# A graph network kernel: a pipelined stage whose first and last passes run only their live operations, and a reordered last stage

## The chip, the cores and the metric

The kernel runs on one core of a Trainium2 chip. The metric is the device time of one launch in microseconds (us). Three launches of the kernel before took 1610.73, 1611.04 and 1617.06 us, so the median is 1611.04 us.

## The reference

The input is a graph of N = 50000 nodes with 128 features each (`x`), and E = 12500 edges (`src`, `dst`, sorted by `dst`) with 128 features each. Two blocks follow each other, each closed by a layer norm over the 128 features:

```
agg  = segment_sum(h[src], dst);  mean = agg / max(deg, 1)
sage(h)  = h @ W_self + mean @ W_neigh + b            # twice, with a relu between them
x1   = layernorm(x + sage(relu(sage(x))))
q,k,v = heads of x1 @ Wq, x1 @ Wk, x1 @ Wv;  e = edge_attr @ We          # H = 4 heads of 128
alpha = (q[dst] . (k[src] + e)) / sqrt(128);  attn = softmax of alpha over the edges of one dst
out  = segment_sum((v[src] + e) * attn, dst) + x1 @ Wskip + bskip
lin  = (layernorm(out) * ln_g + ln_b) @ Wlin + blin
y    = layernorm(x1 + elu(lin + x1))
```

Most nodes have no incoming edge. For them the mean and the attention sum are zero, and the result is a function of the node's own row alone.

## The kernel before, in words

The program has five stages, each a block in which SyncE (SP, issues transfers), GpSimd (POOL), TensorE (PE), ScalarE (ACT) and VectorE (DVE) run their own lists of instructions, with a barrier of all engines between two stages (`phase`, line 1906):

- **setup** (lines 314 to 638): loads and folds the weights, builds index tables from `dst` and `src`.
- **node stage** (`b_sync`, `b_pool`, `b_pe`, `b_act`, `b_dve`, lines 656 to 924): computes every node as if it had no edges, in blocks of 512 rows (NBLK = 98 blocks), and writes `x1` to a table and the final row to the output.
- **A** (line 992 on) and **C** (line 1115 on): the first block of the network for the nodes with edges, 98 tiles of 128 edges in 25 groups.
- **D** (`d_sync` to `d_dve`, lines 1331 to 1903): attention and the output of the nodes with edges, one tile of 128 edges a pass, with scatters over the output's rows; then one last tile for a node whose edges are split between tiles.

The node stage is a software pipeline. A pass `it` works on block `it - lag` in each step; the lags stand in `B_LAG` (line 652) and go from 0 (transpose of the loaded rows) to 6 (the output row `b_o`). NBLK = 98 and the largest lag 6 give TILES = 104 passes. PE, ACT and DVE run them in a hardware loop of 26 turns with four passes in each (lines 707, 753, 800), and in every pass they do every step, also where `it - lag` is no block: such a step works on memory that setup has cleared (lines 363, 515, 635), and its output, where it is stored at all, goes to the tensor `unused` (lines 661 to 680). Every step has a semaphore that starts at CREDIT = 16, so that waits for earlier passes are met at once.

A full pass has, per engine, in this order:

- PE: 4 transposes (L714), 8 products for `y` (L721, L722), 4 transposes of `x1` (L728), one product of 512 columns (L733), 4 products of 256 columns (L739), each wide product in several machine instructions.
- ACT: copy L759, exponential L763, half of the output rows L748, copy L772, relu L776, the other half of L748, Ln L784, Exp L788, and four scaled copies L794 that make `x1`.
- DVE: four sums of squares L807, four statistics L815 for the output (lag 5), clamp L819, four statistics L823 of the y product (lag 1), aggregates L827 and L831, `b_t` L835, `b_w` L839, four `b_z` L844, `b_nm3` L852.
- SP: the load of block `it + 2` (L668), the store of the output block (L672), the store of the `x1` block (L676).
- POOL: `b_x1c` (L880), then indirect transfers: a gather of node rows (L888, passes 0 to 98), and two of the scatters into `redirect` (L894) and, after those, of the look-ups from it (L861); in each sixth pass of the first 96 one of the two is replaced by a gather for stage A (L338). In passes 0, 4, 8, ... 48 it also issues one thirteenth of `dst_row`, the row of all `dst` indices repeated on 128 partitions and cast to 16 bits (L905), and before pass 0 it clears or fills seven tiles (L867 to L872).

In stage D a tile passes through lags too: `a` is the new tile (98 of them), `b` = `a` - 10 the tile whose values are weighted, `c` one behind `b`, `d` two behind. From pass 98 on (`a >= NT`) there is no new tile: this is the drain. In one pass ACT does `turned(c)` (L1591 copy, L1593 square), `exponential(d)` (L1599), `weighted(b)` (L1577, four), L1635, then L1639 and L1641 (the inverse deviation of the output row), L1650 (the output row of `d`), and L1661, L1663 (the inverse deviation for `c`, on which `d_z` L1791 of the next pass waits). DVE's last two steps in a drain pass are `d_nm2` L1830 and `d_var` L1780, and the latter waits for a product of PE (L1457) that stands behind the products L1436 and L1423.

## Time and profile before

| what | us |
|---|---|
| median of three launches | 1611.04 |
| the profiled launch, device time | 1612.87 |
| its span, first to last instruction | 1610.7 |
| setup, to the first load of the node stage | 0 to 34.7 |
| node stage, to the first instruction of stage A | 34.7 to 646.7 |
| stage A | 646.7 to 799.4 |
| stage D's drain and its last tile | 1522 to 1610.7 |

A line of the timeline gives the start in us, the duration in us, the engine, the line, the operation, what it writes and reads, how many instructions are merged in the line, and in brackets how long the engine had been idle before and what ended that. "SPq" and "PEq" are an engine's queue of issued work. An engine that is idle is no loss unless it is the one that the others wait for, so the rows are read for who waits.

### The profile page before, as it was taken

What the parts mean: (1) busy time and instruction counts of PE and PEld (TensorE: products, weight loads), DVE (VectorE), ACT (ScalarE), POOL (GpSimd) and SP (SyncE); (2) the same over time, 40 slices, a digit from 0 to 9 for tenths busy, and PEclk for the clock granted to TensorE, in tenths of its full rate; (3) what the DMA queues carried; (4) which work ended last, traced back from release to release, by engine and by line L of the source; (5) the groups of instructions that cost most, each with busy time, mean ns of one, the idle gap of its engine ahead of it and who ended that gap; (6) DMA issues with size and microseconds to landing.
All of it is one profiled execution on the core that took longest, in us unless ns stands there. A gap on an engine that the chain in (4) does not pass through costs nothing. (4 is left out here: it accounts for less than half of the span.)

```text
span 1610.7 us, 35668 instructions
## 1 busy us (share of the span) xinstructions
PE 1483.8 (92%) x8869; PEld 1135.5 (70%) x8869; DVE 1326.6 (82%) x6248; ACT 1169.2 (73%) x3273; POOL 1036.0 (64%) x1038
## 2 busy tenths in 40 slices
PE   4999999999999998999699977999999999999973
PEld 3777777777777776788566643777777777777763
DVE  5999999999999998566468865788888888888873
ACT  2999999999999998344257751677777777777763
POOL 3788888878888885677367727466566556655421
PEclk9999999999999999999989998999999999999997
DMA  2566666554444443233269963233333333333210
GB/s 80 147 161 159 159 162 162 155 159 150 150 150 150 152 150 119 73 92 92 58 197 288 291 214 97 81 91 91 90 89 87 88 91 90 90 90 88 67 41 6
DMA packets 148429, 199.22 MB, mean 124 GB/s; under 512 B 28399, under 2 KB 71582, under 8 KB 148310
## 3 DMA queue, kind: packets, MB, share of 16 engines
q1 hardware_dynamic: 119690, 160.01, 32.5%
q0 software_dynamic: 27200, 36.26, 10.0%
q10 hardware_dynamic: 1420, 1.60, 0.3%
q8 instruction: 46, 0.75, 0.2%
q14 instruction: 73, 0.60, 0.2%
HBM read 106.66 MB, written 100.07 MB: 128 GB/s over the span
## 5 line engine op out<-in xcount | busy, mean ns | idle before, releaser
L1371 POOL DMA_INDIRECT big<-x_tab,look x196 | 199.8, 1019 | 92.3 <-issue 58.6
L739 PEld LDWEIGHTS pb<-MG_s,big 128*128 128x128 f32 x832 | 149.5, 189 | 126.7 <-ACT big L772 110.5
L1388 POOL DMA_INDIRECT out_dram<-big,idx x98 | 100.5, 1026 | 210.6 <-PE pb L1466 73.4
L739 PE MATMUL pb<-MG_s,big 128*128 128x256 f32 x832 | 207.3, 392 | 24.7 <-ACT big L772 24.6
L748 ACT ACTIVATE big<-big 128x128 f32<-128x128 f32 x416 | 180.2, 482 | 0.0
L721 PE MATMUL pb<-C_s,big 128*128 128x128 f32 x832 | 161.8, 276 | 0.0
L722 PE MATMUL pb<-Ws1c_s,big 128*128 128x128 f32 x832 | 161.8, 276 | 0.0
L880 POOL TENSOR_TENSOR big<-big,cl 128x512 f32<-128x512 f32 x104 | 133.3, 1282 | 36.1 <-DVE big L844 34.0
L1689 DVE CUSTOM_DVE_ANT_0 big<-pb,big,zero 128x128 f32<-128x128 f32 x392 | 119.6, 345 | 38.7 <-PE pb L1511 38.3
L1442 PEld LDWEIGHTS pb<-big 128*128 128x128 f32 x792 | 103.9, 192 | 51.8 <-issue 37.7
L1121 POOL DMA_INDIRECT big<-h1e_tab,hidx x98 | 98.1, 1001 | 60.0 <-issue 35.5
L861 POOL DMA_INDIRECT look<-redirect,idx x98 | 115.8, 1182 | 29.1 <-issue 28.0
L894 POOL DMA_INDIRECT redirect<-idx x98 | 114.7, 1170 | 30.3 <-issue 30.3
L338 POOL DMA_INDIRECT a_xs<-in_x_dram,idx x98 | 100.9, 1029 | 48.3 <-issue 35.9
L722 PEld LDWEIGHTS pb<-Ws1c_s,big 128*128 128x128 f32 x832 | 127.3, 193 | 0.0
L794 ACT ACTIVATE big<-pb,big 128x128 f32<-128x128 f32 x416 | 118.6, 368 | 11.8
L1429 PEld LDWEIGHTS pb<-big,Wskip_s 128*128 128x128 f32 x784 | 101.2, 191 | 36.8 <-issue 36.3
L721 PEld LDWEIGHTS pb<-C_s,big 128*128 128x128 f32 x832 | 127.1, 193 | 0.0
L807 DVE CUSTOM_DVE_ANT_0 big<-pb,big,zero 128x128 f32<-128x128 f32 x416 | 120.5, 346 | 1.9 <-ACTq L265 1.9
L1436 PE MATMUL pb<-big 128*128 128x128 f32 x784 | 112.0, 286 | 5.4 <-ACT big L1577 5.4
L844 DVE SCALAR_TENSOR_TENSOR big<-pb,big 128x128 f32<-128x128 f32 x416 | 116.5, 342 | 0.0
L1442 PE MATMUL pb<-big 128*128 128x129 f32 x792 | 106.4, 277 | 8.4 <-ACT big L1591 5.7
(362 smaller groups left out, 4165.8 us busy)
## 6 DMA issues: line engine op xcount, KB each, us to landing
big<-in_x_dram SPq DMA_DIRECT2D x104, 256.0 KB
x_tab<-big SPq DMA_DIRECT2D x98, 256.0 KB
out_dram<-big SPq DMA_DIRECT2D x98, 256.0 KB, 2.1
c_ve<-ve_tab SPq DMA_DIRECT2D x98, 256.0 KB, 2.6
ve_tab<-c_ve SPq DMA_DIRECT2D x66, 256.0 KB, 3.6
h1e_tab<-a_rows SPq DMA_DIRECT2D x25, 256.0 KB, 2.6
x_tab<-a_rows SPq DMA_DIRECT2D x25, 256.0 KB
big<-in_edge_attr_dram SPq DMA_DIRECT2D x97, 64.0 KB, 1.8
```

What stands on the lines that cost most here:

```text
L721: pe.matmul(o, b_xT[(u - 1) % 2][:, r * P:(r + 1) * P], C_s[:], start=True, stop=False)
L722: t = pe.matmul(o, b_h1T[:, r * P:(r + 1) * P], Ws1c_s[:], start=False, stop=True)
L739: t = pe.matmul(o, b_x1T[:, r * P:(r + 1) * P], MG_s[:], start=True, stop=True)
L748: return act.activation(b_o[u % 2][:, r * D:(r + 1) * D], b_w[u % 2][:, r * D:(r + 1) * D], ACT.Identity, scale=brs3[:, r:r + 1], bias=b_n ...
L794: t = act.activation(b_x1[(u - 1) % 4][:, r * D:(r + 1) * D], PY[(u - 1) % 2][:, r * D:(r + 1) * D], ACT.Copy, bias=1.0, scale=brs1[:, r:r ...
L807: t = v.tensor_tensor_reduce(b_junk[:, r * D:(r + 1) * D], PMG[(u - 3) % 2][r // 2][:, (r % 2) * 256 + 128:(r % 2) * 256 + 256], b_x1[(u - ...
L844: t = v.scalar_tensor_tensor(out=b_z[(u - 3) % 2][:, r * D:(r + 1) * D], in0=PMG[(u - 3) % 2][r // 2][:, (r % 2) * 256:(r % 2) * 256 + 128 ...
L861: g.indirect_dma_start(out=look[:, 0, e:e + 1], out_offset=None, in_=redirect, in_offset=bass.IndirectOffsetOnAxis(ap=idx[:, SRC, e:e + 1] ...
L880: g.tensor_tensor(b_x1c[u % 2].rearrange("p (r d) -> p r d", r=R), b_x1[(u - 2) % 4].rearrange("p (r d) -> p r d", r=R), cl[:].rearrange(" ...
L1371: g.indirect_dma_start(out=o, out_offset=None, in_=x1_tab, in_offset=bass.IndirectOffsetOnAxis(ap=look[:, a, j:j + 1], axis=0), bounds_che ...
L1442: t = pe.matmul(o, hs(ob, h), Wgc_s[:, h, :], start=(h == 0), stop=(h == H - 1))
L1689: return v.tensor_tensor_reduce(hs(junk, h), hs(logit_bank(a), h), d_x1d[a % XD], SCALE, zero[:, 0:1], ALU.mult, ALU.add, d_al[:, H * a + ...
```

## The change

- PE, ACT and DVE run the passes through `all_passes`: passes 0 to 7 and 92 to 103 are written out, with only the steps whose block exists (`present`); passes 8 to 91 stay in a loop of 21 turns of four. A wait for a step is capped at the last value that the step reaches (`due`), and each semaphore's start is raised by the step's lag, in place of the dead steps' increments.
- SP issues no store for a block that does not exist; the tensor `unused` is gone. SP now also waits at the stage's end until `dst_row` has landed.
- POOL runs 102 passes. In passes 2 to 99 it makes `b_x1c`; in every pass it issues three indirect transfers from one list: redirect and node row by turns (198), 16 gathers for stage A, 92 look-ups (91 before).
- The clearings of the node stage's memory are gone from setup (L363, L515, L635, with the waits of L632 and L633). The fills L867 to L872 and the transfers of `dst_row`, now 8 in place of 13 and a small rest, are in POOL's setup, the latter behind a wait for setup's last loads.
- Stage D, passes from 98 on: ACT's square L1593 comes behind the exponential L1599, and the output row L1650 behind L1661 and L1663; DVE's final sum (L1813 to L1821) comes right behind `d_z` and ahead of `d_same` L1798 and the sums L1769.

```diff
-            g.memset(big[:, b_second:b_small_end], 0.0)
+            g.memset(b_mv, 0.0)
+            g.memset(dst_row[:, E:TILES * P], NOWHERE)
+            for k in range(4):
+                g.memset(a_xs[k][:], 1.0)
+            for t in (a_mnT, a_colT, a_colH):
+                g.memset(t[:], 0.0)
+            g.wait_ge(s_ld, 16 * LOADS["later"])
+            part = E // PIECES
+            for k in range(PIECES):
+                at, n = k * part, part if k < PIECES - 1 else E - k * part
+                g.dma_start(dst_row[:, at:at + n], dst[at:at + n].rearrange("(a n) -> a n", a=1).to_broadcast([P, n])
+                            ).then_inc(s_row, 16)
+
+        PIECES = 8
...
-            v.memset(big[:, b_first:b_second], 0.0)
...
-            w("cl")
-            v.wait_ge(s_sa, am["skip"])
-            for b in pb[6:8]:
-                v.memset(b[:].rearrange("p (a d) -> p a d", a=2)[:, :, 0:D], 0.0)
...
+        def b_passes(name):
+            return NBLK + (B_LAG["b_nm3"] - B_LAG[name] if name in ("b_ln", "b_rs") else 0)
+        def present(name, it):
+            return not isinstance(it, int) or B_LAG[name] <= it < B_LAG[name] + b_passes(name)
+        def due(eng, name, value):
+            last = CREDIT + B_LAG[name] + b_passes(name)
+            eng.wait_ge(step(name), min(value, last) if isinstance(value, int) else value)
+        def credit(eng, names):
+            for n in names.split():
+                eng.sem_inc(step(n), CREDIT + B_LAG[n])
...
+        def all_passes(eng, turn):
+            for it in range(4 * EDGE):
+                turn(it, it % 4, it // 4)
+            with eng.Fori(EDGE, LOOPS) as i:
+                for u in range(4):
+                    turn(4 * i + u, u, i)
+            for it in range(4 * LOOPS, PASSES):
+                turn(it, it % 4, it // 4)
...
-                    pe.wait_ge(step("b_h1"), made(B_LAG, "b_h1", it, 1))
-                    pe.wait_ge(step("b_x1"), freed(B_LAG, "b_x1", it, 1, 2))
+                if present("b_py", it):
+                    due(pe, "b_h1", made(B_LAG, "b_h1", it, 1))
+                    due(pe, "b_x1", freed(B_LAG, "b_x1", it, 1, 2))
...
-            for it in range(TILES):
...
+            def move(m):
+                if m < 2 * (NT + 1):
+                    (node_row if m % 2 else redirect_rows)(m // 2)
+                elif m < LOOK_AT:
+                    gather_src(g, (m - 2 * (NT + 1)) // R, (m - 2 * (NT + 1)) % R)
+                else:
+                    if m == LOOK_AT:
+                        for k in range(4):
+                            g.wait_ge(dma_p[k], 16 * len(range(k, NT + 1, 4)))
+                    look_up(g, m - LOOK_AT)
+            for it in range(PASSES - 2):
+                if present("b_x1c", it):
+                    x1c(it, it % 4)
+                for m in range(3 * it, 3 * it + 3):
+                    move(m)
...
+                if live(c) and a < NT:
+                    squared(c)
                 if live(d):
                     exponential(d)
+                if live(c) and a >= NT:
+                    squared(c)
...
-                if live(d):
-                    after(act, "d_nm2", d)
...
+                if live(d) and a < NT:
+                    finished(d)
...
                     act.activation(d_rs[c % 2], d_lw, ACT.Exp, scale=-0.5).then_inc(step("d_rs"), 1)
+
+                if live(d) and a >= NT:
+                    finished(d)
...
+                if live(d) and a >= NT:
+                    final_sum(d)
 
                 if live(b):
                     v.tensor_scalar(d_same[b % 2], dst_row[:, b * P:(b + 1) * P], dst_f[:, b + 1:b + 2], None,
...
-                if live(d):
...
+                if live(d) and a < NT:
+                    final_sum(d)
```

## Rows read from the trace of the kernel before

**Rows 1.** The page, part 1: busy us, share of the span, instructions.

```profile
PE 1483.8 (92%) x8869; PEld 1135.5 (70%) x8869; DVE 1326.6 (82%) x6248; ACT 1169.2 (73%) x3273; POOL 1036.0 (64%) x1038
```

**Rows 2.** Windows: us, then PE, PEld, DVE, ACT, POOL busy (count), PEclk, DMA, GB/s.

```profile
34.70:47.20 12.50, 9.51 (x49) 8.63 (x50) 5.79 (x33) 5.63 (x15) 9.17 (x14) 0.73 0.46 110
...
605.60:611.40 5.80, 5.56 (x37) 4.48 (x36) 5.69 (x34) 5.49 (x15) 4.68 (x4) 1.00 0.43 144
```

**Rows 3.** The timeline, setup's end and the start of the node stage.

```profile
33.24 0.55 DVE L635 MEMSET pb<- 128x256 f32 x2
...
34.72 0.81 SPq L688 DMA_DIRECT2D big<-in_x_dram  x2
34.80 0.77 POOL L867 MEMSET dst_row<- 128x812 uint16 x1 [26.35 <-POOLq L1922]
```

**Rows 4.** The timeline, pass 0 of the node stage.

```profile
37.69 1.11 PE L714 MATMUL pb<-ident,big 128*128 128x128 f32 x4 [5.01 <-DMA big<-in_x_dram]
...
38.59 0.63 PE L721 MATMUL pb<-C_s,big 128*128 128x128 f32 x2
...
39.26 0.69 ACT L759 ACTIVATE big<-pb,vcol 128x512 f32<-128x512 f32 x1 [7.57 <-PE pb L714]
...
42.01 1.06 PE L728 MATMUL pb<-ident,big 128*128 128x128 f32 x4
...
42.86 1.10 PE L733 MATMUL pb<-big,Ws_s 128*128 128x512 f32 x2
...
43.80 1.95 PE L739 MATMUL pb<-MG_s,big 128*128 128x256 f32 x8
...
46.08 1.14 ACT L794 ACTIVATE big<-pb,big 128x128 f32<-128x128 f32 x4
...
47.20 0.34 DVE L807 CUSTOM_DVE_ANT_0 big<-pb,big,zero 128x128 f32<-128x128 f32 x1
```

**Rows 5.** The timeline, pass 98 of the node stage, and the start of pass 99.

```profile
605.68 0.35 DVE L807 CUSTOM_DVE_ANT_0 big<-pb,big,zero 128x128 f32<-128x128 f32 x1
...
606.36 0.86 ACT L748 ACTIVATE big<-big 128x128 f32<-128x128 f32 x2
...
607.61 0.89 DVE L823 BATCH_NORM_STATS2 big<-pb 128x6 f32<-128x128 f32 x4
...
609.13 0.31 ACT L784 ACTIVATE big<-big,eps 128x12 f32<-128x12 f32 x1
...
610.33 1.12 DVE L844 SCALAR_TENSOR_TENSOR big<-pb,big 128x128 f32<-128x128 f32 x4
...
611.44 0.34 DVE L807 CUSTOM_DVE_ANT_0 big<-pb,big,zero 128x128 f32<-128x128 f32 x1
```

**Rows 6.** The timeline, POOL in the same pass.

```profile
605.85 1.28 POOL L880 TENSOR_TENSOR big<-big,cl 128x512 f32<-128x512 f32 x1 [0.31 <-DVE big L844]
```

**Rows 7.** The timeline, the end of the node stage and the start of stage A.

```profile
637.85 0.34 SPq L672 DMA_DIRECT2D out_dram<-big  x1
...
639.83 0.32 SPq L676 DMA_DIRECT2D unused<-big  x1
...
646.71 2.14 DVE L959 TENSOR_SCALAR a_same<-dst_row,dst_f,rdeg 128x128 f32<-128x128 uint16 x8 [6.41 <-PEq L1922]
```

**Rows 8.** DMA queues between 41 and 43 us: packets, MB, share of 16 engines.

```profile
q0 software_dynamic: 192, 0.23, 81.7%
```

**Rows 9.** The timeline, stage D, from the end of one drain pass to the next.

```profile
1559.82 0.49 ACT L1650 ACTIVATE big<-big 128x128 f32<-128x128 f32 x1 [0.23 <-DVE big L1830]
...
1560.31 0.22 DVE L1780 TENSOR_SCALAR big<-pb,big 128x1 f32<-128x1 f32 x1 [0.53 <-PE pb L1457]
...
1561.00 0.58 ACT L1591 ACTIVATE big<-pb 128x512 f32<-128x512 f32 x1
...
1565.74 0.22 DVE L1780 TENSOR_SCALAR big<-pb,big 128x1 f32<-128x1 f32 x1 [0.53 <-PE pb L1457]
```

**Rows 10.** The timeline, PE's first work behind setup's last loads.

```profile
19.13 1.57 PEld L442 LDWEIGHTS pb<-ident,big 128*128 128x128 f32 x8 [2.08 <-DMA Wv_s<-in_L_gnn_Wv_dram]
```

## The prediction before the run

> **What bounds the kernel now.** I read the page's busy shares first: TensorE is busy 92% of the span [rows 1], but that is an average over stages, and the change touches three of them: setup's end, the whole node stage, and the drain of stage D. So I read stretch by stretch. In a steady pass of the node stage the windows view shows 5.80 us with VectorE busy 5.69 of them, TensorE 5.56, ScalarE 5.49, GpSimd 4.68 [rows 2]. VectorE is the bound: its pass goes from 605.68 to 611.44 [rows 5] without a gap, 5.76 us. From pass 1 at 47.20 [rows 4] to pass 99 at 611.44 [rows 5] are 98 passes in 564.24 us, again 5.76 each. So the passes at both ends, where most steps are dead, cost as much as the full ones. Pass 0 is dearer: TensorE starts at 37.69 and VectorE's pass 1 at 47.20 [rows 4], with a mean granted clock of 0.73 between 34.70 and 47.20 [rows 2], so part of that stretch ran at 1.2 GHz. At the far end the last real output is stored at 637.85, a dead store follows at 639.83, and stage A begins at 646.71, 6.88 us behind it [rows 7].
>
> **Part 1: the last passes of the node stage.** Up to pass 98 VectorE has all its steps. What is live after that, taking pass 99's start as 611.44 [rows 5]:
> Pass 99 and pass 100 lose the statistics of line 823 (0.89 [rows 5]): 4.87 each. That reaches 621.18. In them `b_z` still waits for ScalarE's Ln and Exp, whose inputs are ready as before.
> Pass 101 has no sums of squares (four L807; the first is 0.35 and the gaps make 1.1 of them) and no `b_z` (1.12 [rows 5]). What remains is bound by ScalarE: the exponential, four output rows at 0.43 each (two took 0.86 [rows 5]), Ln 0.31 [rows 5], Exp about 0.2, then `b_nm3`: 0.7 + 1.75 + 0.5 + hand-offs of 0.2 = 3.15, to 624.3.
> Pass 102: output rows 1.75, Ln, Exp, `b_nm3`: 2.65, to 627.0. Pass 103: the last four output rows and the hand-off, 2.1, so the last store is issued at 629.1 in place of 639.83. **The end of the stage comes 10.7 us earlier.** What follows the last store (landing, barrier, 6.88 us) is unchanged. GpSimd must be done by then: it has `b_x1c` until pass 99, at about 611.6, then nine transfers at some 1.3 us each, so it ends near 625, ahead of 629.1. It is the cover of this term; were it later, the gain would shrink by as much.
>
> **Part 2: the first passes.** VectorE has a full pass only from pass 5. It can start it when TensorE has given the last product (L739) of block 2 in pass 4. Before, pass 3 started at 47.20 + 2 x 5.76 = 58.7 and pass 5 at 70.2. Now block 0 goes through alone. Its chain to the end of its L739: transposes 1.11, copy 0.69, wide product (about 2.0 at 1.2 GHz; it took 1.10 in a stretch where the clock rose), relu 0.7, the y products at 1.2 GHz 3.42 (from 38.59 to 42.01), statistics and aggregate 1.25, Ln and Exp 0.5, L794 1.14, the next copy 0.7, transposes 0.5, wide product 1.0, L739 1.95 [rows 4, 5]: 15.0, and eleven hand-offs at 0.15 make 16.6. From a start at 38.0 (part 3) that ends at 54.6 where pass 3 used to start at 58.7. Passes 3 and 4 then run at TensorE's pace, 5.56 of work [rows 2] and a wait for the copy, about 5.8 each, so pass 5 starts at 66.4 in place of 70.2: **3.8 us gained**. Bounds: if the clock is at 2.4 GHz before the y products, they take half of 3.42 and the gain is 5.5; if it stays at 1.2 GHz through L739 as well, about 3 us more go and the gain is 0.8.
> Here a rule speaks against the change. The rows show the dead products of pass 0 keeping TensorE at work (9.51 busy in 12.50 [rows 2]) until the clock had risen. The Trainium skill's page "TensorE: Matmul & The Clock Gate" (Part 1) says that the throttled state is the default and that activity releases it. By that rule, dropping the dead products leaves gaps, and the rise comes later; that is the lower bound above.
>
> **Part 3: setup.** VectorE's clearing of 0.55 at 33.24 [rows 3] stands ahead of the two copies with which it ends setup, and GpSimd, idle for 26.35 us by then [rows 3], and SP wait for that end. So the node stage's first load is issued 0.55 earlier, at 34.17. The other clearings stood in idle time and give nothing. GpSimd's fills at the stage's start (L867 at 34.80 [rows 3] and the six after it) hid behind the load and pass 0; moved into setup they hide in those 26 us. The eight transfers of `dst_row` can be issued from 19.13, when the last loads have landed [rows 10]. They are the cost here: they move 8 x 128 rows of 3 KB. The nearest row is one of the 13 old pieces, in a window of 2 us with 0.23 MB at 81.7% of the engines [rows 8]; 3.2 MB at that rate is 3.2 / 0.23 x 2 x 0.817 = 23 us of all engines, less some for the gather in that window, say 17 to 23. From about 20.5 that ends between 37.5 and 43.5, and the first load of `x` (landed 2.97 us after its issue before [rows 3, 4]) runs beside it. Bounds: no delay, or the pieces first, 5 us. I take 0.85, near the lower end, because the load comes when the pieces are three quarters done, and a single piece left the engines some room (18.3% [rows 8]); so TensorE starts at 38.0. If the issue of the pieces blocks GpSimd until its queue drains, setup ends some 2 us later; that is inside the upper bound.
> In the Trainium skill, "DMA: Bandwidth & Descriptors" (Queues, rings and completion order) says that each engine takes the queues' packets in turns. By that, a load beside a larger queue is slowed but never held to the queue's end: the rule is nearer to my value than to 5.
>
> **Part 4: the steady passes.** GpSimd issues three indirect transfers a pass as before, and no piece of `dst_row`. It waits 0.31 for VectorE in each pass [rows 6], so nothing of this is on the path: 0. One look-up fewer in stage A: TensorE runs that stage to its end, 0. The written-out passes cost instructions to fetch only; stages A, C and D are written out already and show no stall for it: 0.
>
> **Part 5: the drain of stage D.** The loop that sets a drain pass runs from `d_var` at 1560.31 to `d_var` at 1565.74, 5.43 us [rows 9]: Ln and Exp, ScalarE's copy L1591 at 1561.00, square, exponential, the four weightings, then TensorE's L1436, L1423 and L1457, for which `d_var` waits (0.53 idle behind L1457). The output row L1650 (0.49) lies ahead of `d_var`, in ScalarE's idle time [rows 9]. The change puts it behind the Exp, which is inside that loop: every pass in which the weightings set the pace gets 0.4 to 0.5 longer. These are passes 98 to 104, seven of them: +3.0. In passes 105 and 106 other waits are longer; in the last three the final sum itself is the path, and the earlier exponential gives back what the output row costs, about 0. The earlier final sum on VectorE helps nobody in the seven passes: its result was not waited for. **Stage D gets 3.0 us longer.** Bounds: -3, if the final sum's wait is the loop in more passes than I see, to +5, if `d_same`, now behind it, also holds up L1436.
>
> **The sum.** -10.7 - 3.8 (setup's 0.55 and the load's 0.85 are in it) + 3.0 = -11.5. Against the profiled launch, 1612.9, that is 1601.4; the median of the launches is 1.8 lower, so I expect 1611.0 - 11.5 = **1599.5 us**. A change under 0.5%, 8.1 us, can't be told from none, so "faster" means below 1603.0.
>
> **Rivals.**
> *The drain of D is no slower or gains* (chance 0.2). For it: the reordering takes ScalarE's square out of the exponential's way, and VectorE's idle time ahead of `d_var` shows that it has room. Against it: `d_var` waits for TensorE, not for the sum. Part 5 becomes 0 to -3: 1593.5 to 1596.5.
> *The start gives nothing* (0.13): the `dst_row` pieces hold the first loads back by 3 to 5 us, or TensorE stays at 1.2 GHz into pass 3. For it: the engines were full at 81.7% with a single piece [rows 8]. Part 2 and 3 go to +0.5: 1603.8.
> *GpSimd becomes the bound of the node stage* (0.04), and the kernel is slower. A transfer that stands at another place in the pass than now may take longer there. GpSimd's slack is 0.31 a pass [rows 6] and about 98 passes pay what exceeds it. The break-even with 11.5 us is 0.12 over the slack, that is 0.43 more in a pass; at 0.55 more, 98 x 0.24 = 23.5, and the time is 1623.
> *The dead passes were not on the path* (0.03), because GpSimd's 102 passes of three transfers set the stage's end: then only setup and the fill are left: 1610.
>
> **How the numbers follow.** My case has 0.6. Its own bounds, 5.5 or 0.8 at the start and +2 to +4 in D, give 1597 to 1603.5. To hold 8 in 10 the range takes in the gaining drain at one end and half of the lost start at the other: 1594 to 1604. Faster by over 0.5%: my case but for its last twentieth, and the gaining drain: 0.8. Within 0.5%: most of the lost start, the lost drain: 0.16. Slower: 0.04.
>
> **What would show it.** After the change VectorE's passes 6 to 98 must still be 5.76 apart; the last store of the node stage must come 17.7 us after the start of pass 99, and pass 5 about 28.5 us after TensorE's first transpose. The first L714 should start near 38.0; a later start is the `dst_row` traffic. In D, `d_var` to `d_var` should be 5.8 to 5.9 in place of 5.43, with L1650 between L1663 and L1591. The prediction is wrong if a steady pass has changed at all, if GpSimd is the last to end the node stage, or if D's drain got shorter.

## The result and the profile after

The changed kernel takes **1607.0 us** in the median of seven launches (1605.4 to 1607.65), the kernel before 1611.04; the ratio is **0.996** with a 95% interval of 0.9946 to 0.9974. So it is faster, by 4.0 us and not by 11.5, and 1607.0 lies outside the range of 1594 to 1604. (By the prediction's own measure, below 1603.0 for "faster", it counts as unchanged; the interval is narrower than that measure.) The profiled launch took 1605.4 with a span of 1603.6, 7.1 under that of before. The spans can be taken apart, the medians can't. The medians are closer than the spans because the profiled launch of before was 1.8 above the median of its kernel and that of after 1.6 below.

Where the 7.1 went, from one mark to the next in both traces:

| from, to | before | after | difference | forecast |
|---|---|---|---|---|
| span's start to TensorE's first transpose of `x` | 37.69 | 42.97 | +5.28 | +0.3 |
| to VectorE's pass 5 (its sums of squares) | 32.53 | 26.92 | -5.61 | -4.1 |
| to pass 99 | 541.22 | 541.36 | +0.14 | 0 |
| to stage A | 35.27 | 23.64 | -11.63 | -10.7 |
| stages A and C | 317.93 | 317.74 | -0.19 | 0 |
| stage D to the end | 646.06 | 650.97 | +4.91 | +3.0 |

(Pass 5 started at 70.22 before and at 69.89 after; D started at 964.64 and 952.63.) The page's busy shares of after, against [rows 1], show the dead steps gone, 204 of TensorE's machine instructions among them (six passes of 34):

```profile
PE 1458.1 (91%) x8665; PEld 1113.7 (69%) x8665; DVE 1291.4 (81%) x6053; ACT 1138.2 (71%) x3197; POOL 1018.0 (63%) x1026
```

**Setup.** The timeline of after around setup's end, of three engines, and TensorE's first transpose; it answers to [rows 3] and [rows 4].

```profile
19.85 4.54 POOL L363 DMA_DIRECT2D dst_row<-in_dst_dram  x8 [12.84 <-DMA Wv_s<-in_L_gnn_Wv_dram]
...
33.66 0.25 DVE L635 COPY rdeg<-pb 128x104 f32<-128x104 f32 x1
...
39.80 0.82 SPq L717 DMA_DIRECT2D big<-in_x_dram  x2
...
42.97 1.11 PE L742 MATMUL pb<-ident,big 128*128 128x128 f32 x4 [9.83 <-DMA big<-in_x_dram]
```

VectorE ends setup at 33.9, as expected, and GpSimd has issued its eight pieces by 24.4. Yet SP loads only at 39.80. What stands between is the barrier: the view by source of the line that ends a block (L1972 after), between 15 and 45 us. The columns are the least, middle and longest duration in ns and the first and last start.

```profile
L1972 POOLq EVENT_SEMAPHORE  x2: 17/17/17, 39.3 to 39.4; - x2
L1972 POOLq DRAIN  x1: 16406/16406/16406, 22.8 to 22.8; - x1
...
L1972 DVEq DRAIN  x1: 773/773/773, 33.2 to 33.2; - x1
```

A drain (DRAIN) is the instruction with which each engine ends a block, ahead of the barrier. GpSimd's lasts 16.4 us, to 39.2, and everybody waits for it. The view by source of L363 gives the pieces' time from issue to landing; the last, issued at 23.7, landed at about 38.8:

```profile
DMA to landing us min/median/max: 4.9/10.2/15.1
```

**The node stage's start.** TensorE ran at 1.2 GHz until about 50.0: the same wide product took 2.08 at 44.86 and 1.02 at 50.82. The start gained all the same (-5.61).

```profile
44.86 2.08 PE L764 MATMUL pb<-big,Ws_s 128*128 128x512 f32 x2 [0.78 <-ACT big L793]
...
50.82 1.02 PE L764 MATMUL pb<-big,Ws_s 128*128 128x512 f32 x2
```

**The node stage's end.** First the ends of the kernel before (view by source, line L1911, 600 to 650 us), then of after (L1972, 600 to 640). GpSimd's last look-up ended at 638.38 before and at 624.85 after.

```profile
L1911 POOLq EVENT_SEMAPHORE  x2: 17/17/17, 646.0 to 646.1; - x2
L1911 POOLq DRAIN  x1: 10172/10172/10172, 635.8 to 635.8; - x1
...
L1911 SPq DRAIN  x1: 7/7/7, 642.1 to 642.1; - x1
```

```profile
L1972 POOLq EVENT_SEMAPHORE  x2: 17/17/17, 634.2 to 634.3; - x2
...
L1972 POOLq DRAIN  x1: 17907/17907/17907, 616.2 to 616.2; - x1
...
L1972 SPq DRAIN  x1: 7/7/7, 631.7 to 631.7; - x1
```

In both kernels SP had its last store landed before the stage ended, by 3.9 us before and 2.4 after. GpSimd's drain ended last, 7.6 behind the last look-up before and 9.3 after. SP issued its last store at 629.2 (view by source of L700), 18.0 behind the start of pass 99; 17.7 was forecast. In the last passes the timeline and the windows of after show the clock fall as well; the columns of the windows are those of [rows 2].

```profile
607.57 1.99 PE L771 MATMUL pb<-MG_s,big 128*128 128x256 f32 x8 [1.54 <-ACT big L809]
...
613.33 3.65 PE L771 MATMUL pb<-MG_s,big 128*128 128x256 f32 x8 [1.78 <-ACT big L809]
```

```profile
605.49:611.25 5.76, 2.90 (x16) 2.10 (x15) 5.65 (x34) 4.40 (x12) 4.67 (x4) 1.00 0.26 94
611.25:617.12 5.87, 3.94 (x11) 2.42 (x9) 4.77 (x26) 4.09 (x10) 4.64 (x5) 0.71 0.25 90
```

**The drain of D.** One pass of after, timeline, against [rows 9]. In the loop now: ScalarE's output row L1648 behind the Exp L1714, VectorE's `d_same` (L1868) behind the final sum (L1839 to L1847), TensorE's summed product L1476 idle for it, then L1463, L1497 and `d_var`.

```profile
1546.23 0.29 ACT L1712 ACTIVATE big<-big,eps 128x1 f32<-128x1 f32 x1 [2.16 <-DVE big L1834]
...
1546.67 0.48 ACT L1648 ACTIVATE big<-big 128x128 f32<-128x128 f32 x1
...
1548.43 1.13 ACT L1617 ACTIVATE big<-pb,big 128x128 f32<-128x128 f32 x4
...
1549.46 0.26 DVE L1868 TENSOR_SCALAR big<-dst_row,dst_f 128x128 f32<-128x128 uint16 x1
...
1549.77 1.16 PE L1476 MATMUL pb<-big 128*128 128x128 f32 x8 [0.88 <-DVE big L1868]
...
1552.01 0.22 DVE L1834 TENSOR_SCALAR big<-pb,big 128x1 f32<-128x1 f32 x1 [1.14 <-PE pb L1497]
```

The period is 6.03 in place of 5.43. But not every pass kept to it. Windows of after from `d_var` to `d_var`, then the pass with the last tile's preparations (105 to 106), which took 7.90 before:

```profile
1520.46:1527.87 7.41, 5.66 (x29) 4.22 (x28) 4.10 (x15) 4.02 (x15) 1.46 (x2) 0.80 0.12 43
1527.87:1533.91 6.04, 4.74 (x31) 3.86 (x31) 3.92 (x15) 3.81 (x14) 1.47 (x2) 0.97 0.19 55
...
1558.05:1567.34 9.29, 6.05 (x28) 4.54 (x27) 5.10 (x22) 3.82 (x14) 1.46 (x2) 0.73 0.02 7
```

The work is the same, the granted clock is not: 0.80 in the pass of 7.41. Such a pass, ahead of pass 105 and with a clock near 0.8, is called a slow pass below. From pass 105 to 106 the clock was lowered before the change too, 0.78 in its window.

### The profile page after: what moved, and what is told of

Same layout as the page of the kernel before. It is cut to its first block and busy times, and to the rows that moved or that the text cites. A ratio compares the mean times of both kernels' runs of the same rounds, so it can differ in the third digit from the quotient of the medians.

```text
span 1603.6 us, 34874 instructions
## 1 busy us (share of the span) xinstructions
PE 1458.1 (91%) x8665; PEld 1113.7 (69%) x8665; DVE 1291.4 (81%) x6053; ACT 1138.2 (71%) x3197; POOL 1018.0 (63%) x1026
## 5 line engine op out<-in xcount | busy, mean ns | idle before, releaser
L771 PEld LDWEIGHTS pb<-MG_s,big 128*128 128x128 f32 x784 | 141.8, 191 | 119.5 <-ACT big L809 103.9
L771 PE MATMUL pb<-MG_s,big 128*128 128x256 f32 x784 | 197.0, 394 | 24.9 <-ACT big L809 24.7
L782 ACT ACTIVATE big<-big 128x128 f32<-128x128 f32 x392 | 169.6, 483 | 0.5 <-DVE big L906 0.5
L750 PE MATMUL pb<-C_s,big 128*128 128x128 f32 x784 | 152.6, 276 | 0.3 <-ACT big L814 0.3
L751 PE MATMUL pb<-Ws1c_s,big 128*128 128x128 f32 x784 | 152.2, 276 | 0.0
L1743 DVE CUSTOM_DVE_ANT_0 big<-pb,big,zero 128x128 f32<-128x128 f32 x392 | 119.3, 344 | 37.2 <-PE pb L1551 36.9
L930 POOL TENSOR_TENSOR big<-big,cl 128x512 f32<-128x512 f32 x98 | 124.8, 1274 | 34.2 <-DVE big L896 27.9
L944 POOL DMA_INDIRECT big<-in_x_dram,idx x98 | 111.6, 1139 | 25.5 <-issue 25.1
L750 PEld LDWEIGHTS pb<-C_s,big 128*128 128x128 f32 x784 | 119.7, 193 | 1.0 <-ACT big L814 0.9
L1476 PE MATMUL pb<-big 128*128 128x128 f32 x784 | 113.0, 288 | 7.9 <-DVE big L1868 7.9
L751 PEld LDWEIGHTS pb<-Ws1c_s,big 128*128 128x128 f32 x784 | 119.8, 193 | 0.0
L850 DVE CUSTOM_DVE_ANT_0 big<-pb,big,zero 128x128 f32<-128x128 f32 x392 | 113.4, 344 | 3.4 <-PE pb L771 3.4
```

The lines of the kernel that those rows point to most:

```text
L750: pe.matmul(o, b_xT[(u - 1) % 2][:, r * P:(r + 1) * P], C_s[:], start=True, stop=False)
L751: t = pe.matmul(o, b_h1T[:, r * P:(r + 1) * P], Ws1c_s[:], start=False, stop=True)
L771: t = pe.matmul(o, b_x1T[:, r * P:(r + 1) * P], MG_s[:], start=True, stop=True)
L782: return act.activation(b_o[u % 2][:, r * D:(r + 1) * D], b_w[u % 2][:, r * D:(r + 1) * D], ACT.Identity, scale=brs3[:, r:r + 1], bias=b_n ...
L850: t = v.tensor_tensor_reduce(b_junk[:, r * D:(r + 1) * D], PMG[(u - 3) % 2][r // 2][:, (r % 2) * 256 + 128:(r % 2) * 256 + 256], b_x1[(u - ...
L930: g.tensor_tensor(b_x1c[u % 2].rearrange("p (r d) -> p r d", r=R), b_x1[(u - 2) % 4].rearrange("p (r d) -> p r d", r=R), cl[:].rearrange(" ...
```

## Experiments

Five groups of runs, on five chips. On three of the chips (e5 to e14, e19, e20) every kernel took 1640 to 1675 us: stages A and C were longer there (A 168 us and more in place of 152), the node stage was not. So ratios are compared within a group, and single stages by their traces. D's drain is counted over the last thirteen periods of `d_var` (to pass 108), and the rest behind the last `d_var`. Before: 74.37 and 27.22; after: 82.48 and 24.98.

### e1: the pieces of `dst_row` out of setup

```diff
@@ setup, GpSimd
-            for k in range(PIECES):
-                g.dma_start(dst_row[:, at:at + n], ...).then_inc(s_row, 16)
@@ b_pool, ahead of b_x1c
+                if it % 4 == 0 and 2 <= it // 4 < 2 + PIECES:
+                    g.dma_start(dst_row[:, at:at + n], ...).then_inc(s_row, 16)
```

> The changed kernel, but GpSimd issues the eight transfers of dst_row in passes 8, 12, ... 36 of the node stage and not in setup. Theory A: GpSimd's drain at setup's end (22.8 to 39.2) waits until the last piece has landed and holds every engine there; without them setup's last event is VectorE's at 33.7, SP issues the first load of x at 34.1 to 34.3 in place of 39.8, and the kernel takes 5.1 to 5.6 us less than the changed one: 1601.7. Rival A1: the pieces cost nothing by their drain, something else in setup holds the barrier (the issue of the pieces ends at 24.4): the first load stays near 39.8 and the time near 1607. Rival A2: the pieces, issued in the node stage, cost GpSimd more than its slack there, and the passes that hold one get longer: the first load is at 34.2, but the stage gives back 0.3 to 1 us a piece, and the time is 1604 to 1607.

Ratio 0.9932 (0.9916 to 0.9947). The first load is issued at 35.14, and the node stage is as long as before the edit (595.0 from first load to stage A; 595.1 in the changed kernel). GpSimd's drain of setup is now over at 7.1, 0.09 behind its last fill; the barrier opens at 34.6 behind VectorE:

```profile
L1972 POOLq EVENT_SEMAPHORE  x2: 17/17/17, 34.6 to 34.7; - x2
L1972 POOLq DRAIN  x1: 3491/3491/3491, 3.6 to 3.6; - x1
...
L1972 DVEq DRAIN  x1: 771/771/771, 33.8 to 33.8; - x1
```

Theory A holds: 4.7 us in the trace, and the ratio is better than that of the changed kernel by 0.0028, 4.5 us. (The profiled launch itself had three slow passes in D, which took 3.3 us more than in the trace of after.)

### e20: half of the pieces

```diff
-            for k in range(PIECES):
+            for k in range(4):                 # the other four in the node stage, as in e1
```

> The changed kernel with four of the eight pieces of dst_row in setup and four in the node stage. Theory A: GpSimd's drain ends when its last piece has landed; four pieces, issued from 19.9, land by about 30, ahead of VectorE's end of setup at 33.9, so they are hidden whole: first load at 34.2 to 35.2, and 4.5 to 5 us less than the changed kernel, ratio 0.993. Rival A3: any piece in setup makes the drain longer by a fixed time behind the last issue: then the first load comes at about 37 to 38.

First load at 34.99; GpSimd's drain (L1978 in this kernel) ends at 31.8:

```profile
L1978 POOLq DRAIN  x1: 10370/10370/10370, 21.4 to 21.4; - x1
```

Four pieces are hidden whole, eight are not. Rival A3 is out: the drain ended 9.3 behind the end of the last issue, and 14.8 with eight pieces, so it is no fixed time. The DMA view has the last bytes of the pieces moved by 31.0 here and by 38.5 with eight, each time under 1 us ahead of the drain's end. Ratio 0.9909 (0.9882 to 0.9936).

### e3 and e11: what ends the node stage

```diff
-        B_MOVES = 3 * (PASSES - 2)
+        B_MOVES = 3 * (PASSES - 2 - 2)
-                for m in range(3 * it, 3 * it + 3):
+                for m in range(3 * it, min(3 * it + 3, B_MOVES)):
```

> The changed kernel, but GpSimd's last six look-ups (those of its last two passes of the node stage) are issued in stage A instead; the same 128 are made. Theory C: what ends the node stage is GpSimd's drain, some 9.2 us after its last transfer has been issued (624.85 to 634.1), not SP's last store; six look-ups fewer at 1.3 us move that drain 7 us ahead, SP's own end at 631.6 takes over, and the stage ends 2.4 us earlier. Stage A has GpSimd idle for about 11 us at its end and keeps its 153.3. Time: 1604.6. Rival C1: SP's last store and its landing set the end and GpSimd's drain only waits for the others: stage A starts at 634.9 as now, 1607.0. Rival C2: the look-ups in stage A come too late for that stage's own last ones, its GpSimd drain at 768 to 775 moves past 787, and what the node stage gains is lost there: 1607 to 1610.

Ratio 0.9938 (0.9922 to 0.9953). Node stage 592.45 in place of 595.09, stage A 152.8 in place of 153.3. The ends of the blocks in this kernel:

```profile
L1972 POOLq EVENT_SEMAPHORE  x2: 17/17/17, 630.2 to 630.3; - x2
L1972 POOLq DRAIN  x1: 12543/12543/12543, 611.4 to 611.4; - x1
...
L1972 SPq DRAIN  x1: 7/7/7, 630.1 to 630.1; - x1
```

GpSimd's drain ends at 623.9, 9.0 behind its last look-up, and SP's last store is now the path. Theory C holds to 0.25 us. The same on the kernel before, with eight look-ups:

```diff
-        B_LOOKS = 2 * TILES - 4 * R - LOOK_AT
+        B_LOOKS = 2 * TILES - 4 * R - LOOK_AT - 8
-                    elif t >= LOOK_AT:
+                    elif LOOK_AT <= t < LOOK_AT + B_LOOKS:
```

> The kernel before, with GpSimd's last eight look-ups (the two in each of its last four passes) issued in stage A instead; the dead passes and all else as before. Theory C: what ends the node stage of the kernel before is GpSimd's drain, about 7.6 us after its last look-up has ended (638.38 to 646.0), while SP is ready at 642.1. Without transfers in its last four passes GpSimd's drain has nothing to wait for after about 619, SP's end takes over, and stage A begins 3 to 4 us earlier, its length unchanged; 0.2% of the time. Rival C3: the drain takes some 7.6 us behind any last instruction of GpSimd, also behind its last dead addition at about 636.5; then the stage ends 1 to 2 us earlier. Rival C1: SP's stores set the end, nothing changes.

The node stage is 608.61 from first load to stage A, 3.4 shorter than 611.99. But GpSimd's drain still ended it: it took 7.0 us behind the last dead addition, which ended at 635.3, with no transfer issued for 20 us.

```profile
634.05 1.27 POOL L880 TENSOR_TENSOR big<-big,cl 128x512 f32<-128x512 f32 x1 [4.47 <-DVE big L844]
```

```profile
L1911 POOLq EVENT_SEMAPHORE  x2: 17/17/17, 642.3 to 642.4; - x2
```

So here C3 had the mechanism and C the size. What that drain waits for is open: it is not the landing of look-ups, which in the changed kernel landed 2.4 to 3.2 us after their issue. And the whole kernel was *slower*: ratio 1.0055 (1.0025 to 1.0084), 1.004 (1.0009 to 1.0071) when repeated:

> The kernel of e11_before_looks again (the kernel before, its last eight look-ups issued in stage A). Its node stage ended 3.4 us earlier, but it was 9 us slower than before on a chip where stages A and C took 178 and 200 us in place of 152 and 166. Theory K: that loss belongs to such chips, where transfers hold stage A up; where stage A is at 152 to 154 the gain stays and the ratio is 0.997 to 0.999. Rival K1: eight more look-ups in stage A cost more than 3.4 us on any chip: ratio 1.002 or more, stage A over 156.

Neither outcome decides between K and K1 for this kernel, as the repeat met such a chip again. On these chips stage A took 175.2 to 180.7 us in the four traces with moved look-ups (e11, e13, e14, e19) and 167.8 to 174.5 in the six without (e5, e6, e9, e10, e12, e20). Within one chip it was 175.2 to 180.7 against 170.0 (e12), and 179.5 (e19) against 171.5 (e20). With six look-ups moved, on the changed kernel and a chip with a short stage A, it costs nothing (e3, e4, e18). Which wait in stage A grows is open.

### e2: the old order of D

```diff
@@ d_act
-                if live(c) and a < NT:
+                if live(c):
                     squared(c)
@@ the same for finished(d) and, on VectorE, final_sum(d); the three late calls go
```

> The changed kernel with the three moves in the drain of stage D undone (square ahead of the exponential, output row ahead of d_var's Ln, final sum after the squares); all else as changed. Theory B: the reordering alone makes D's drain longer, so d_var to d_var goes from 6.03 back to 5.4, stage D to the span's end from 651.0 to 646.1, and the time is 4.9 us under the changed kernel: 1602.1. Rival B1: my forecast's size was right (3.0) and 1.9 us of D came from something else, such as the missing look-ups or another phase of the loop: 1604. Rival B2: D's drain is longer because of what stage A and C leave behind, not by the order: 1607.

Ratio 0.9915 (0.9899 to 0.993), against 0.996 of the changed kernel. D took 644.1 (646.1 expected): drain 73.93, 26.73 behind it, no slow pass. Theory B holds. Of the 1.9 below the expectation 1.0 is a shorter start of D, which every trace of the changed kernel on such a chip has; the drain was 0.4 shorter, as its stretch from 105 to 106 kept the clock here (7.21 for 7.90), and what follows it 0.5.

### e5, e6, e9: which of the three moves

```diff
@@ e5: output row back              @@ e6: square and final sum back, output row stays moved
-                if live(d) and a < NT:
+                if live(d):
                     finished(d)
@@ e9: VectorE, d_same ahead of the early sum
+                if live(b): d_same
                 if live(d) and a >= NT:
                     final_sum(d)
-                if live(b): d_same
```

> The changed kernel with ScalarE's output row back ahead of d_var's Ln in the drain of D; final sum early and square late stay. The profiled runs so far show this for D's drain: d_var to d_var 5.43 in the old order and 6.03 in the new one; the new order adds 5.0 over the last 22 passes where the clock stays up, takes 2.2 off behind the last d_var, and single passes with a mean granted clock of 0.78 to 0.80 cost 7.41 to 7.61. Theory D: the output row (0.48) behind the Exp is inside the loop and is the larger part; back at its old place it leaves d_same behind the early final sum as the rest, 5.5 to 5.6 a pass, D 644 to 646 against 651.0 and no pass with a lowered clock ahead of pass 105, as TensorE idles less. Rival E: d_same behind the early final sum sets the pass by itself; then the period stays 5.95 to 6.03 and D stays at 648 to 654.

> The changed kernel with the final sum and the square of D's drain at their old places; only the output row stays moved. Theory D: 5.43 + 0.48 = 5.9 a pass, and what the early final sum gives behind the last d_var is lost (27 instead of 25 from the last d_var to the end). Rival E: the output row costs nothing, the period is 5.43.

> The changed kernel with one exchange in VectorE's order in D's drain: d_same ahead of the early final sum. Theory D: TensorE's summed product then waits for ScalarE's weightings instead of d_same, which end 0.2 later than nothing: 5.85 to 5.95 a pass in place of 6.03. Rival E: d_same was what the product waited for (0.89 idle), so the period falls to 5.43 or under.

The shortest period ahead of pass 105 is 5.48 in e5, 5.81 in e6 and 5.82 in e9, against 5.43 before and 6.03 after. So the output row costs 0.39 a pass alone (e6), and `d_same` behind the final sum 0.2 on top of it (6.03 - 5.82, e9) but only 0.05 without it (e5). Behind the last `d_var` it takes 24.98 in e9, 26.43 in e5 and 26.5 in e6: the 2.2 us gained there need both the early final sum and the late output row. Theory D holds for the periods. The late square was not tried by itself; it goes with the final sum here. e6 has a slow pass, so the moved output row alone is enough for one:

```profile
1571.35:1578.98 7.63, 5.92 (x30) 4.48 (x29) 4.09 (x14) 4.08 (x15) 1.46 (x2) 0.78 0.14 42
```

Ratios: 0.9923 (0.9891 to 0.9955), 0.9924 (0.9895 to 0.9953) and 0.994 (0.9912 to 0.9968); too close to tell apart.

### e10: TensorE kept at work in the drain

```diff
+                if a >= NT:
+                    for k in range(5):
+                        pe.transpose(PB[:, 0:P], ident[:], ident[:])
                 if live(c):
                     products(c)
@@ the same five ahead of summed(b)
```

> The changed kernel with ten dead transposes of the identity on TensorE in each pass of D's drain, five ahead of the products and five ahead of the summed product, where it waits 0.88 and 0.89 now; they write a bank that nothing reads. Theory F: single passes of 7.4 to 7.6 and the 9.3 of pass 105 are TensorE's clock falling to 1.2 GHz because it idles some 30% of the pass; with the fillers every pass up to 104 takes 6.03 to 6.1, pass 105 takes 8 or less, and D's span is 646 to 648. Rival F1: the clock falls in spite of the activity, D stays between 648 and 654. Rival F2: the fillers are longer than the waits they stand in and add 0.2 or more a pass.

Periods to pass 105: 6.66, 6.05, 6.05, 6.04, 6.04, 6.04, 6.03, 6.04; pass 105 to 106 is 7.43 and the drain 77.83. The windows of an ordinary pass and of that one:

```profile
1585.05:1591.09 6.04, 5.38 (x40) 4.43 (x40) 3.79 (x13) 3.73 (x13) 1.46 (x2) 1.00 0.19 55
1609.20:1616.63 7.43, 5.27 (x38) 4.23 (x37) 5.12 (x23) 3.82 (x14) 1.47 (x2) 1.00 0.03 9
```

The clock is 1.00 in both; the fillers stand in the waits and cost nothing. For the stretch from 105 to 106 theory F is well borne out: all five traces with fillers (e10, e13, e14, e17, e18) have a clock of 1.00 there, and of the fifteen without only e2 has, the others 0.70 to 0.83. For slow passes one trace can't tell, as e3, e9 and e12 have none either, without fillers in the drain; none of the five filled traces has one. D took 650.8, not the expected 646 to 648; on such chips 3 us go ahead of the first `d_var`. Ratio 0.9934 (0.9912 to 0.9956). The same stretch in the old order, first as e2 took it, then e11:

```profile
1551.97:1559.18 7.21, 4.15 (x28) 3.24 (x27) 4.95 (x22) 4.32 (x15) 1.46 (x2) 1.00 0.03 9
1625.87:1634.94 9.07, 6.02 (x28) 4.54 (x27) 4.94 (x22) 4.33 (x15) 2.46 (x3) 0.73 0.02 6
```

### e12: TensorE kept at work at the node stage's start

```diff
+                if it == 0: ten dead transposes        # ahead of the wait for the first block
                 ...
+                if it < 2: four, ahead of b_ph, and four at the pass's end
```

> The changed kernel with dead transposes of the identity on TensorE at the node stage's start: ten while the first block of x is on its way, four in each of the waits ahead of the wide product and at the end of passes 0 and 1. Theory G: the first passes ran at 1.2 GHz until about 7 us after the first transpose (a wide product 2.08 in place of 1.02, four transposes 1.11 in place of 0.60) because TensorE had idled since 33.9; with activity the clock is up by the first blocks, and from TensorE's first transpose of x to VectorE's pass 5 it takes 24 to 25 us in place of 26.9. Rival G1: the fillers do not bring the clock up earlier, 26.9 or 0.5 more.

From the first transpose (43.09) to pass 5 (68.62) it took 25.53 in place of 26.92. The wide product of pass 0 still took 1.69, the next one, at 49.72, 1.02. The fillers began only 2.2 us ahead of the first transpose, since the barrier holds TensorE as well. But the same stretch took 25.8 to 27.0 in the ten other traces without these fillers (25.77 in e6, 27.04 in e3), and 25.9 (three times) and 26.8 in the four later traces with them (e13, e14, e17, e18). So no gain is shown, and G and G1 stay undecided. Ratio 0.995 (0.9926 to 0.9975), within the error of the changed kernel's.

### e15 and e16: the two kernels again, on one chip

> The kernel before, unchanged, for its trace on the chip of this comparison. It is set against itself: ratio 1.000 within 0.3%. By the given trace: node stage 612.0 from the first load, D's drain 74.4 over the last thirteen passes, 27.2 behind the last d_var. If this chip's gathers are slower, stage A is 165 us or more in place of 152, and nothing of the other two changes.

> The changed kernel, unchanged, for its trace on the same chip. Ratio 0.996. The terms against the kernel before: first load +4 to +5.5, first transposes to pass 99 -5.5, pass 99 to stage A -11.6 (-10 to -12), D's thirteen passes +5 with no pass at a lowered clock ahead of pass 105 and 1.4 to 1.6 more for each such pass, -2.2 behind the last d_var. If a term depends on the chip, it shows as one outside these.

Before against itself 0.9988 (0.9976 to 1.0); after 0.9957 (0.9942 to 0.9972), ten launches from 1601.62 to 1610.87. D in this trace of after took 654.43 where the first took 650.97; its windows from pass 99 on:

```profile
1519.81:1527.52 7.71, 5.95 (x30) 4.48 (x29) 4.08 (x14) 4.03 (x15) 1.46 (x2) 0.78 0.13 41
1527.52:1533.57 6.05, 4.53 (x31) 3.70 (x31) 3.92 (x15) 3.81 (x14) 1.48 (x2) 1.00 0.26 55
1533.57:1541.27 7.70, 5.95 (x30) 4.55 (x30) 3.78 (x13) 3.73 (x13) 1.46 (x2) 0.78 0.14 45
1541.27:1547.31 6.04, 4.29 (x30) 3.43 (x30) 3.89 (x12) 3.73 (x13) 1.48 (x2) 1.00 0.15 53
1547.31:1554.99 7.68, 5.91 (x31) 4.60 (x31) 4.13 (x16) 3.81 (x13) 1.46 (x2) 0.78 0.02 8
```

Three slow passes here, three in e1, one in the first trace of after, one in e20, none in e3 and e12, all with this order of D. Each costs 1.4 to 1.7. In a slow pass TensorE does what it does in the others; it idles 1.7 of the 6.0 us of an ordinary pass of this order, and 1.2 of 5.4 in the old one. The expectation "no pass at a lowered clock" was wrong for e16. In the old order none of six traces (before, e2, e4, e11, e15, e19) has one. So the new order costs a varying amount: the drain is 79.2 to 85.8 in six traces of it. The old order varies less, 73.9 to 76.8, nearly all of it from pass 105 on.

### e4, e13, e14, e17, e18: versions that beat both

e4 joins e1, e2 and e3. e13 joins e1, e3, e9, e10 and e12, and puts the output row behind Ln and Exp only in the last three passes with a `d_var`. e14 adds an exchange in the drain:

```diff
@@ d_pe
+                if live(c) and a >= NT:
+                    squares(c)
                 if live(b + 1) and a >= NT - 1:
                     values(b + 1)
-                if live(c) and a >= NT:
-                    squares(c)
@@ d_dve: value_sum(b) behind d_z in the drain too
```

> The changed kernel with all three: dst_row's pieces in the node stage, the drain of D in its old order, and the last six look-ups in stage A. By theories A, B and C together the terms add up, as they lie in different stages: 5.1 + 4.9 + 2.4 = 12.4 less than the changed kernel, 1594.6. If the terms are right but one is absorbed by a later barrier, the sum falls short by that term: 1597 to 1600. If A1, B2 and C1 hold, 1607.

> All that the runs pointed to, on the changed kernel: dst_row's pieces in the node stage, the last six look-ups in stage A, the fillers at the node stage's start, and in D's drain d_same ahead of the early final sum, the output row ahead of d_var's Ln but in the last three passes that have one, and ten dead transposes a pass. Against the changed kernel: -5.1 for setup, -2.4 for the node stage's end, -2 at its start, and D at 641 to 643 in place of 651 (5.43 to 5.5 a pass, pass 105 at 7.2 to 7.4, 25 behind the last d_var). Sum about -18: ratio to the kernel before 0.985. If the terms of D don't add up (the fillers cost what they give, or the early sum delays the product), 0.988, as with the old order of D.

> As the run with all that the runs pointed to, and one exchange more in D's drain: TensorE issues the row variance's product ahead of the next values, and VectorE computes z ahead of the sum of values. Theory H: the values' product (1.02) stands between the summed product and d_var in the loop that sets the pass, so a pass takes 4.6 to 4.9 in place of 5.43, 5 to 8 us less over the drain. Rival H1: the squares' reduction on VectorE is later than the summed product's end and takes the place of the values' product; then a pass is 5.2 to 5.4 and the gain under 2 us.

> As e14_swap, but GpSimd's last six look-ups stay in the node stage. Theory J: on a chip where the gathers bound stage A, six look-ups more there cost 6 to 8 us (about 1.3 each), more than the 2.4 to 4 that the node stage gains; this kernel is then 3 to 5 us faster than the one with moved look-ups, with stage A at 168 to 172 against 175 to 178, and its ratio to before is 0.983 to 0.985. Rival J1: stage A's length varies from execution to execution by more than the look-ups cost; the two kernels agree within 2 us.

> The kernel of e14_swap again, on the same chip as the three others. Theory J: ratio about 0.987 as before, 3 to 5 us over e17_swap_no_looks. Rival J1: equal to it within 2 us, or 2 us faster, by what the node stage's end gains.

e4 takes 1591.05, ratio **0.9876** (0.9858 to 0.9895): the terms add up within the error (0.0084 under the changed kernel's 0.996; e1, e2 and e3 alone have 0.0028, 0.0045 and 0.0022), with a node stage of 592.2 and D at 645.1. e13: 0.9917 (0.9895 to 0.9939), short of its 0.985. D took 648.8 for the expected 641 to 643, but 3.1 of that are ahead of the first `d_var` (53.2 for 50.0), as on such chips in other traces too (53.3 in e5, 53.1 in e14), and stage A took 180.7. e14: 0.9866 (0.9826 to 0.9907), drain **69.44**, 6.35 less than e13, period 4.85: theory H holds, the product of the next values stood in the loop between the summed product and `d_var`. (The run has both exchanges; which gives how much is not shown.) e17 and e18 on a chip with short stages A and C: 1587.88 and 1586.5, ratios **0.9835** (0.9808 to 0.9862) and **0.9834** (0.9808 to 0.986). There the moved look-ups cost nothing in stage A (153.2 against 153.5) and give 2.65 in the node stage, and the kernels agree within 2 us, as J1 said. J spoke of a chip with a long stage A, which this was not, so it stays untested. The window of a drain pass of e18, in which TensorE is now busy all the time, its ten dead transposes included; whether they have become a cost is not tested:

```profile
1531.23:1536.08 4.85, 4.85 (x39) 4.37 (x39) 4.04 (x15) 3.91 (x14) 1.55 (x2) 1.00 0.04 12
```

## Why the prediction was wrong

The sum's deviation in the spans is +4.4 us (-7.1 for -11.5). By steps:

**Part 3 failed, and is the larger error (+5.0).** I priced the eight pieces by the load that runs beside them, 0.85, with 5 as the bound, and let GpSimd's end of setup be its issue of them. The run showed that the load did not share the engines with the pieces at all: it was not issued before they had landed, since the block's end holds GpSimd until then (16.4 us of drain, e1, e20). TensorE's first transpose came at 42.97 and not at 38.0. My estimate of when the pieces would land was right, 37.5 to 43.5 against 38.8; I had the number and asked only what it does to the load's speed. The sentence on a blocking issue was near, with a price of 2. That the engines share between queues, which the Trainium skill's "DMA: Bandwidth & Descriptors" (Queues, rings and completion order) states, was not tested: first load and pieces never ran together. The load took 3.17 from issue to first transpose, 2.97 before. The 0.55 of VectorE's clearing can't be seen: its drain of setup ended at 32.4 in e3, 34.0 in after and 35.3 in e18.

**Part 5: the output row was sized about right, the clock was missing.** Without slow passes (e3) the new order costs 5.05 over the drain. Of these 3.9 are in the eight periods up to pass 105, where I had 3.0: the output row gives 0.39 a pass, and `d_same` behind the final sum, which I had only as a bound, another 0.2. From 105 to 106 go 1.1 more (8.99 for 7.90), at a lowered clock in both (0.81 and 0.78); at 1.00 the stretch took 7.21 in the old order (e2) and 7.43 in the new one (e10). The new order gives 2.24 behind the drain, and D's start is 0.9 shorter in the traces of the changed kernel, which I don't explain; together 1.9. I had 3.0, by 0.4 to 0.5 in seven passes and nothing else. The rest of the first trace's +4.91, 3.1 us, are one slow pass, a longer pass 105 and a longer 106, all at a lowered clock. In e16 it is 6.4. Part 2 weighed the rule that an idle TensorE gets the lower clock, and Part 5 lengthened passes in which TensorE idles over a quarter of the time without asking the same question. The Trainium skill's "TensorE: Matmul & The Clock Gate" (Part 1) says that activity releases the throttle; by that rule filled waits keep the clock, and e10 agrees: 1.00 with them, 7.43 in place of 9.29.

**The medians.** They differ by 4.0 and not by 7.1, and for launches without a trace the cause is open. Slow passes are a likely part of it: the ten launches of e16 go from 1601.62 at a mean clock of 0.970 to 1610.87 at 0.963. But the launches of the kernel before on that chip, whose trace (e15) has no slow pass, spread nearly as far, from 1610.12 at 0.979 to 1617.48 at 0.974.

**Part 2: right, under-sized by 1.5.** The fill gave 5.6 in place of 4.1. Pass 5 came 26.9 behind the first transpose, 28.5 was forecast; 5.5 was my upper bound. Pass 3 started 15.7 behind the first transpose for my 16.6, and passes 3 and 4 took 5.7 and 5.5 for my 5.8. The clock did stay at 1.2 GHz for the first block, and came up at the end of its y products, not behind them. In other traces the same stretch took 25.8 to 27.0, so the gain varies by over 1 us with the moment of the rise.

**Part 1: size right, mechanism wrong.** The stage's end came 11.6 earlier for 10.7. SP's last store came as forecast. But "what follows the last store is unchanged" was not what set the end: in both kernels GpSimd's drain did, 9.3 behind its last look-up after the change. That GpSimd is the last to end the node stage was one of the prediction's own signs of being wrong; it was so before the change already, which I had not looked at. I had GpSimd done "near 625" as the cover of this term, and it was, at 624.85. Its cover lacked the 9.3 of the drain, and ended at 634.1, not 625. It cost 2.5 to 2.65 against what SP allowed (e3, e18). By luck of the same mechanism the kernel before had waited 3.9 for it.

**Rivals.** "The start gives nothing" came nearest: it put the start at +0.5, and first transpose and fill together came to -0.3; its change of -7.2 meets the -7.1 of the spans. Its first cause was the right one (the pieces, 5), its second was not (the clock was up before pass 3). That it meets the spans so closely is in part luck, as D took 1.9 more than its 3.0 and the stage's end 0.9 less. The steady pass stayed at 5.76, and A and C at the same sum, as forecast.

## What to carry to other kernels

A transfer moved into a stage is to be priced to its landing, not to its issue, where the stage ends with a barrier: here the drain of GpSimd held every engine, so issue such transfers where another engine's work outlasts them, or behind the barrier. Look first for who ends a stage in the kernel as it is. In a drain of a pipeline, write down the loop that sets its pass, and move an instruction into it only if nothing in it waits; an instruction taken out of it (a product for the next pass) is worth its time in each. Where a reordering or the removal of dead work makes TensorE idle, look at the granted clock of those stretches in more than one execution, and try dead products in the waits. Before a gain of 1 us is put down to an edit, look how far the same stretch varies between traces without it (e12).

## What the runs showed of the hardware

GpSimd's drain at the end of a block was short only where the block had issued no transfer: 0.09 us behind the last fill of setup in e1, 0.05 in the kernel before. Where transfers had been issued it was long whatever came last: 7.0 us behind a plain addition, 20 us after the last transfer had been issued (e11), 7.4 at stage A's end of the changed kernel, 7.6 to 9.3 behind a look-up, and until landing (16.4) with broadcast, casting transfers underway. It ends the program as well: in the changed kernel it is over at 1603.4 of 1603.6, 8.9 behind the last scatter, while the other engines were done by 1592.8. The drains of VectorE, ScalarE and TensorE took 0.02 to 3.7. The pieces, 3.1 MB written to 128 partitions, needed 19 us from first issue to last landing. And the clock falls in single passes of equal work, alternating with passes at 1.00, in one execution three times and in another not at all.
